# Attention scores of two heads: each head's products on its own 64 partitions, the two heads' banks alternated block by block, keys copied once

## The reference, cut to what matters

```
scores = jnp.einsum('bhqd,bhkd->bhqk', q, k) * scale
attn = jax.nn.softmax(scores + causal, axis=-1)      # sparsemax in the last layer
ctx = jnp.einsum('bhqk,bhkd->bhqd', attn, v_c)
```

## Time and profile before

| what | before |
|---|---|
| median of three runs | 3157.74 us (3154.28 to 3167.81) |
| the profiled execution | 3140.92 us, span 3139.4 us |
| busy share of the span | PE 89%, PEld 72%, DVE 70%, ACT 51%, POOL 48% |
| mean granted TensorE clock | 0.958 of full speed |
| instructions | PE 20990, DVE 6269, ACT 3388, POOL 2213 |

### The profile page before, as it was taken

The page is one execution under the profiler, slowest core; times in us unless marked ns, Lnnn a source line. Parts: engine busy times, 40 slices in busy tenths (PEclk is TensorE's granted clock), DMA queues, the critical chain, the costliest instruction groups (busy, mean ns, idle before and its releaser), DMA issues. The chain is left out here.

```text
span 3139.4 us, 61420 instructions
## 1 busy us (share of the span) xinstructions
PE 2800.3 (89%) x20990; PEld 2273.6 (72%) x20990; DVE 2186.6 (70%) x6269; ACT 1613.7 (51%) x3388; POOL 1513.7 (48%) x2213
## 2 busy tenths in 40 slices
PE   3878699999999999969988889898799999999996
PEld 2555478889899889846666666666588888888864
DVE  4787778788788778757787777766645555454576
ACT  1545444444454444545665555565455555555553
POOL 3587853443343353385656666322233333332487
PEclk8878799999999999989999999999899999999998
DMA  2465678788888888422334343210466666666345
GB/s 82 158 237 178 225 258 311 282 289 307 286 290 308 289 291 309 169 40 55 95 98 107 105 107 106 94 67 23 162 207 215 221 217 212 204 240 203 125 95 125
DMA packets 212009, 580.14 MB, mean 185 GB/s; under 512 B 24617, under 2 KB 146417, under 8 KB 167409
## 3 DMA queue, kind: packets, MB, share of 16 engines
q1 hardware_dynamic: 174832, 525.03, 47.7%
q0 software_dynamic: 36864, 51.14, 8.0%
HBM read 450.14 MB, written 125.96 MB: 184 GB/s over the span
## 5 line engine op out<-in xcount | busy, mean ns | idle before, releaser
L1173 POOL TENSOR_TENSOR al<-t,ah 128x512 fp32r<-128x512 f32 x220 | 284.2, 1292 | 879.3 <-ACT ah L1407 879.3
L544 PE MATMUL bank<-xh,gu 128*128 128x256 f32 x3520 | 675.8, 292 | 33.6 <-DVE gc L1678 25.0
L544 PEld LDWEIGHTS bank<-xh,gu 128*128 128x128 f32 x3520 | 516.1, 191 | 57.6 <-issue 53.8
L1864 DVE TENSOR_REDUCE st<-bank 128x1 f32<-128x512 f32 (+3 forms) x1024 | 421.7, 480 | 157.6 <-PE bank L605 151.8
L1504 ACT ACTIVATE pt<-bank 128x512 f32<-128x512 f32 (+1 forms) x1152 | 510.9, 540 | 25.6 <-PE bank L608 22.9
L587 PE MATMUL bank<-masks_bf,ident_bf 128*128 128x128 bf16 x1896 | 431.2, 251 | 101.0 <-DVE st L1864 38.3
L605 PE MATMUL bank<-ksT,qsT 128*128 128x512 f32 (+3 forms) x1536 | 409.8, 368 | 5.6 <-DVE top L1862 3.1
L1512 ACT ACTIVATE oT<-bank 128x512 f32<-128x512 f32 x192 | 114.6, 597 | 574.4 <-PE bank L684 574.4
L587 PEld LDWEIGHTS bank<-masks_bf,ident_bf 128*128 128x128 bf16 x1896 | 169.9, 98 | 311.1 <-DVE st L1864 96.3
L608 PE MATMUL bank<-qaT,ksT 128*128 128x512 f32 (+3 forms) x1536 | 389.2, 370 | 0.0
L544 PE MATMUL bank<-xl,gu 128*128 128x256 f32 x1760 | 353.5, 282 | 0.0
(11 more groups left out here) (254 smaller groups left out, 5266.9 us busy)
## 6 DMA issues: line engine op xcount, KB each, us to landing
gu<-wu_scratch SPq DMA_DIRECT2D x110, 1032.0 KB, 5.1
gu<-wu_scratch SPq DMA_DIRECT2D x110, 1024.0 KB, 7.4
dn<-wd_scratch SPq DMA_DIRECT2D x110, 1024.0 KB, 6.6
xs<-xs_scratch SPq DMA_DIRECT2D x110, 264.0 KB, 4.4
ys_scratch<-yb SPq DMA_DIRECT2D x110, 256.0 KB, 6.9
raw<-in_gu SPq DMA_DIRECT2D x16, 1024.0 KB, 6.7
wu_scratch<-hi SPq DMA_DIRECT2D x16, 1024.0 KB
wu_scratch<-lo SPq DMA_DIRECT2D x16, 1024.0 KB
```

What stands on the lines that cost most here:

```text
L544: mm = pe.matmul(bank[:, TS * h:TS * (h + 1)], gu[:, col:col + P], x[s % 2][:, TS * k:TS * (k + 1)], start=(n == 0), stop=(n == len(terms) ...
L1173: pool.tensor_tensor(em["al"][s % 2][:, m, :], em["t"][g % 2][:, :], em["ah"][s % 2][:, m, :].bitcast(F32), ALU.subtract).then_inc(al_read ...
L1864: ins = dve.reduce_max(st[:, 0, r:r + 1], bank[:, first:first + width], AX.X)
```

## The change

1. The unit tables are interleaved: both heads' 512-wide units, then both heads' 384 + 128 units, then both 256-wide ones.
2. `scores` takes units two at a time (`both`): it waits for both banks, adds both masks, and then issues the products block by block, head 0 and head 1 in turn, each into its own bank, and each with the 64 rows of its own head (`rows`).
3. The calls in pairs with experts take two units and then four (`FORE = 2`) where they took three and three, on PE, ACT and DVE alike.
4. `ksT` is one tile for each pair without zero rows, filled by one copy of 128 rows on ACT; the semaphore `k_half` and four memsets of the setup go.
5. `masks_last` is asked by the place in the plan; it holds for the q form of the same pairs. With it the masks follow each couple of units, where they followed each three.
6. POOL's `clear` waits for the last two units, one for each head.

```diff
-for _j in range(2):
-    Q_UNITS += [[(_j, 3, 0, 512)], [(_j, 2, 0, 384), (_j, 0, 384, 128)], [(_j, 1, 0, 256)]]
-    K_UNITS += [[(_j, 0, 0, 512)], [(_j, 3, 0, 128), (_j, 1, 128, 384)], [(_j, 2, 0, 256)]]
+for _q, _k in (([(3, 0, 512)], [(0, 0, 512)]),
+               ([(2, 0, 384), (0, 384, 128)], [(3, 0, 128), (1, 128, 384)]),
+               ([(1, 0, 256)], [(2, 0, 256)])):
+    Q_UNITS += [[(_j, *_b) for _b in _q] for _j in range(2)]
+    K_UNITS += [[(_j, *_b) for _b in _k] for _j in range(2)]
 NU = len(Q_UNITS)
+FORE = 2
...
-                    for u in units:
-                        name = (which, G, u)
-                        S.add(name, "dve" if which == "q" else "act")
-                        if S.former[name]:
-                            pe.wait_ge(*S.former[name])
...
+                    for u in units[::2]:
+                        both = (u, u + 1)
+                        for v in both:
+                            name = (which, G, v)
+                            S.add(name, "dve" if which == "q" else "act")
+                            if S.former[name]:
+                                pe.wait_ge(*S.former[name])
                         if not bare and not masks_last:
-                            mask(u, True)
...
+                            for v in both:
+                                mask(v, True)
+                        last_mm = {}
+                        for n in range(len(table_of[u])):
...
+                            for v in both:
+                                j, blk, first, width = table_of[v][n]
+                                rows = slice(SW * j, SW * (j + 1))
+                                to = S.bank((which, G, v))[:, first:first + width]
+                                if which == "q":
+                                    last_mm[v] = pe.matmul(to, mem["qsT"][rows, P * blk:P * (blk + 1)],
+                                                           keys[rows, 0:width], start=begin, stop=end,
+                                                           skip_group_check=True)
...
-                    scores("k", G, range(NU // 2))
+                    scores("k", G, range(FORE))
...
-                    pool.wait_ge(s_act, S.count[("k", G, NU // 2 * (j + 1) - 1)])
+                    pool.wait_ge(s_act, S.count[("k", G, NU - 2 + j)])
...
-                    act.activation(keys[0][0:SW, :], bank[0:SW, :], ACT.Copy).then_inc(k_half, 1)
-                    act.activation(keys[1][SW:P, :], bank[SW:P, :], ACT.Copy).then_inc(x_act, 1)
+                    act.activation(mem["ksT"][key_at[G] % 2][:, :], X.bank(f"Tk{G}")[:, :], ACT.Copy).then_inc(x_act, 1)
```

More of the change, by code:

```diff
@@ L578, in scores @@
                     mem = mems[kinds[G // NP]]
+                    keys = mem["ksT"][key_at[G] % 2]
                     bare = which == "k" and G in plan
-                    masks_last = which == "q" and len(S.banks) == len(units)
+                    masks_last = which == "q" and G - 1 in plan
                     side = 0 if which == "q" else 1
+                    table_of = Q_UNITS if which == "q" else K_UNITS
                     def mask(u, start):
-                        unit = (Q_UNITS if which == "q" else K_UNITS)[u]
+                        unit = table_of[u]
                         diag = min(first + (P * blk if which == "q" else 0) for _, blk, first, _ in unit)
@@ L598, in scores @@
                         if not bare and not masks_last:
-                            mask(u, True)
-                        for n, (j, blk, first, width) in enumerate(unit):
+                            for v in both:
+                                mask(v, True)
+                        last_mm = {}
+                        for n in range(len(table_of[u])):
                             begin = n == 0 and (bare or masks_last)
[L602 to L614, removed]
+                            end = n == len(table_of[u]) - 1 and not masks_last
+                            for v in both:
[6 more added lines that the diff above has]
+                                                           skip_group_check=True)
+                                else:
+                                    last_mm[v] = pe.matmul(to, keys[rows, P * blk:P * (blk + 1)],
+                                                           mem["qaT"][rows, T - width:T], start=begin, stop=end,
+                                                           skip_group_check=True)
@@ L616, in turn_rows @@
+                        for v in both:
+                            if masks_last:
+                                last_mm[v] = mask(v, False)
+                            last_mm[v].then_inc(s_full, 1)
                 def turn_rows(n):
@@ L666, in keys_in @@
                     pe.wait_ge(x_act, X.count[f"Tk{G}" if key_pair(G) == G else f"Tq{G}"])
-                    pe.wait_ge(k_half, key_at[G] + 1)
                 def outputs(G):
@@ L809, in pair_with_experts @@
                         turn_rows(n + 1)
-                    scores("k", G, range(NU // 2, NU))
+                    scores("k", G, range(FORE, NU))
                     if is_at(n - 1, "spm") and p == 1:
@@ L1550, in pair_with_experts @@
                     experts(G, 0)
-                    probabilities(G, range(NU // 2))
+                    probabilities(G, range(FORE))
                     highs()
@@ L1556, in pair_with_experts @@
                         take_rows(n + 1)
-                    probabilities(G, range(NU // 2, NU))
+                    probabilities(G, range(FORE, NU))
                     if is_at(n - 1, "spm") and p == 1:
@@ L2304, in build @@
         "qsT": at("qsT", [P, T], F32R),
-        "ksT": [[at(f"ksT{i}{j}", [P, T], F32R) for j in range(2)] for i in range(2)],
+        "ksT": [at(f"ksT{i}", [P, T], F32R) for i in range(2)],
         "qaT": at("qaT", [P, T], F32R),
```

14 lines of the change are left out of this document (5 added, 9 removed).

## The result

The changed kernel takes 3428.43 us (median of 4 runs, 3423.27 to 3432.94) against 3156.95 us (median of 4): a ratio of **1.0857**, 95% interval 1.0843 to 1.0871.

What follows compares the result with a forecast made beforehand. PE's queue was taken to bound the expert stages and gqa; 70 + 76 + 119 - 25 - 25 = +215 us on the median 3157.7 gave 3373 us, ratio 1.068, range 3250 to 3465.

Steps and rivals of the forecast that it cites:

- What bounds it: PE's queue sets the time in mla with experts, spm with experts and gqa; PE busy 29.8 of 31.3 us in mla.
- Pairs alone, +70: Waits for readers before the third couple and tiling changes: k form +0.41, q form +0.35 us, times 92 pairs.
- spm with experts, +76: Last couple waits for the bank just filled: k form +1.18, q form +0.78 us, times 39 pairs.
- mla with experts, +119, less 25 for `gc`: PE waits for late readers, 4.1 us times 29 pairs; PE's 25.0 us wait for `gc` should vanish in exchange.
- Copies of keys, -25: One ACT copy fewer per key tile, counted only where PE waits: 0.59 us off each of 42 waits.
- mla alone, counted as nothing: 21 pairs where DVE and POOL are as busy as PE (264.1 of 345.4 us): no effect counted.
- Change of tiling: Between 128-row masks and 64-row products: 0.18 us in, 0.09 out, 0.10 load laid open, from 8-row matmuls.
- Full overlap of row halves: Both heads' products on 64 rows run at once, saving 1280 columns of streaming, 0.53 us a form.
- rival of serial halves: Row halves run one after another in the couples: 57 + 20 us more, giving 3450; chance 0.12.
- free changes: Tiling changes cost nothing at 64 rows: 80 + 37 us less, giving 3256; chance 0.11.
- slack: Waits in pairs with experts fall into slack: 170 us would go, leaving about 3200; chance 0.05.
- the faster side: Halved streaming in 384 forms (205 us) and 25 for copies, with no wait in exchange: 2930; chance 0.06.

Runs made afterwards that it cites:

- e6: Kernel with both mends (e5), but in pairs alone the q form's first four masks stand ahead of both couples: 3189.44 us, ratio 1.0106.
- e9: Kernel with both mends (e5), but each mask added in two passes on the head's own 64 rows: 3177.29 us, ratio 1.0054.
- e5c: Kernel with both mends (e5), but the keys' copy done in two halves of 64 rows: 3221.12 us, ratio 1.0193.
- e10: Kernel with both mends (e5), but outputs between the couples only from pair 50 on, so not in mla alone: 3196.44 us, ratio 1.0112.
- e2: Kernel before, with its order and calls, but products of 64 rows and one copy of keys: 3610.51 us, ratio 1.1507.
- e1: Changed kernel's order and calls, but products of 128 rows on padded keys with two key copies: 3343.88 us, ratio 1.0666.
- e12: Kernel with both mends (e5), but products of 128 rows on padded keys with two key copies: 3163.54 us, ratio 1.0021.
- e3: Changed kernel, but with experts three units a call (couple and single, then single and couple), masks behind each q-form call: 3231.63 us, ratio 1.0314.
- e8: Kernel before, with outputs moved in pairs alone behind the fourth unit of q and k forms, as in e4: 3162.82 us, ratio 1.0014.
- e4: Changed kernel, but in pairs alone outputs (q form) and transposes of outputs (k form) stand ahead of the third couple: 3326.81 us, ratio 1.0623.
- e5: Changed kernel with both mends, those of e3 and e4 together: 3188.28 us, ratio 1.0091.

## Why the prediction was right, and where its sizes were off

The forecast was 3373 us, the result 3428.43: the sign, the mechanism and the range held, the sum was +215 and the truth +271. That the range held is in part luck: the two things that the forecast had left out, the clock and mla alone, each put some 27 us on top, and nothing in the range had been set aside for either. Step by step:

**What bounds it.** PE's queue in the stages with experts and in gqa. Confirmed for the stages with experts: PE's idle time there grew by 140 us, where the three rows of waits are 159 and the waits for `gc` became 15 shorter. In pairs alone e6 and e9 show that DVE is close behind.

**Pairs alone, +70.** Measured: gqa +55.4, the stretches of 14 +21.1, the pairs between +0.6, so +77. The medians over gqa, from a form's first start to the next operation's, are 2.73 us for q and 2.56 for k (forecast 2.63 and 2.45), and 2.35 and 2.03 before. ACT's first read of a k form comes 0.81 us after the form's start by the median, forecast 0.84. In the k form shown it has the copy `oT` (0.60 us) ahead of `pt` and begins at 1.31. The 1.93 us that the prediction sets against 1.39 as reading are the moment of release, counted from the form's start; the reading itself is 1.09.

**spm with experts, +76.** Measured +68.7. The second calls take 1.73 us (k) and 2.07 (q) on the mean, forecast 1.88 and 2.20; the first ones 0.44 and 0.54, forecast 0.58 and 0.67. The four calls of a pair take 4.78 us together where they took 3.46 (the same places in the trace of before, 0.66 a k call and 1.07 a q call on the mean), and 1.32 x 39 is 51 us; the other 17 lie outside these calls and were not taken apart.

**mla with experts, +119, less 25 for `gc`.** The stage grew by 118, net. Second calls 2.25 (k) and 3.09 us (q), forecast means 2.4 and 3.4, the first ones 0.43 and 0.53: 6.30 us where 2.96 were, and 3.34 x 29 is 97 us. The waits for `gc` fell by 15, not 25. The clock was 0.96 in this stage where it had been 0.99, by which its 865.5 us of PE work would take 865.5 x (0.99/0.96 - 1) = 27 us more, an estimate; PE was in fact busy 42 us longer. So the forms were over-sized and the clock not seen. The net term, 119 - 25, was short by 24 us.

**Copies of keys, -25.** The waits that name the copy fell from 31.5 to 15.1 us, not below 10 as was forecast, so by these waits the term is 16 us and not 25. By e5c, though, the 160 copies are worth 33 us in the mended kernel, of which only 19 are in waits that name them. The step that was too narrow is "count only where PE waits for the copy". A copy also delays what stands behind it in ACT's queue; that the rest lies there is likely and was not shown.

**mla alone, counted as nothing.** +27 us, of which part is scatter, as e10 says.

**Change of tiling.** I took 0.18 in, 0.10 of load laid open and 0.09 out, from 8 rows. At 64 rows the medians over gqa tell it cleanly (us from start to start):

| step | 128 rows | 64 rows | kernels |
|---|---|---|---|
| one mask of 128 columns to the product | 0.039 | 0.160 | before, e2 |
| one mask of 256 columns to the product | 0.039 | 0.213 | before, e2 |
| product of 512 columns to the next mask | 0.322 | 0.434 | before, e2 |
| couple of 512, both heads, to the next mask | 0.552 | 0.434 | e1, after |
| the second product of a couple behind the first | 0.315 | 0.003 | e1, after |

In: 0.12 to 0.17, out: 0.11, together 0.23 to 0.29 where I had up to 0.37. The Trainium skill, "TensorEngine Tiling", Key Properties, says that a change of mode drains the engine; the trace is in keeping with it, and this table is what a change costs here. e9 confirms it from the other side: with masks on 64 rows the couple of 512 goes to the next mask in 0.322 us, 0.11 less.

**Full overlap of row halves.** It holds: a couple takes as long as one of its products alone, 0.434 us. The rival of serial halves is out, as are free changes (the table), slack (the stages with experts grew by 187 us, 140 of it PE standing idle) and the faster side. The Trainium skill, "TensorE: Matmul & The Clock Gate", Part 3, has tiles on different row groups start about 4 ns apart; here it is 3.

**What I did not see: at once is also late.** Take the steps of gqa's forms in the changed kernel and in e1, the same order on 128 rows, with their waits left out: three couples of masks and three of products in turn (medians; where a step ends in a wait, the same step of a kernel in which it does not, e2's single products for 64 rows and e12's couples for 128). A k form on 64 rows is 0.216 + 0.434 + 0.323 + 0.486 + 0.202 + 0.315 = 1.98 us, on 128 rows 0.094 + 0.551 + 0.150 + 0.659 + 0.081 + 0.322 = 1.86; a q form is 0.205 + 0.434 + 0.322 + 0.430 + 0.202 + 0.316 = 1.91 against 0.084 + 0.552 + 0.148 + 0.702 + 0.081 + 0.411 = 1.98. So the overlap pays for the changes of tiling in the q form, and not in the k form.

And the first bank of a couple is full later, since both fill together behind the change of tiling: ACT's first read of gqa's k forms comes 0.81 us after the form's start, 0.67 in e1, 0.63 before; DVE's in the q forms 0.78, 0.64, 0.61. All that waits for that reader is later by as much. This is the likely reason for most of the distance between 10.95 us a gqa pair in the changed kernel and 10.38 in e1: the medians of the forms are longer by 0.15 (q) and 0.26 (k), 26 of the 36 us. The rest is in keeping with the clock, 0.93 against 0.97: the outputs, 1.20 us by the median in both, took over 1.8 us in 17 of 64 pairs, and in 7 of e1's. It was argued from these starts, not tested alone.

## What to carry to other kernels

Before two streams are interleaved on a ring of banks, count the units between a bank's filling and its next use: four units on a ring of three put a wait for the reader, 0.8 us in the forms shown, on PE in every form, and taking or covering these waits gave back 7.7 of the 8.6%. Splitting the calls so that each bank waited for was filled in the call before took most of it back. Row halves at once save streaming and are paid for with changes of tiling around every mask; from these figures one would expect them to win where the passes between changes are long, and where PE, not the reader of its banks, sets the pace. No run here shows such a win: even e9, with no change of tiling inside a form, is 0.5% above the kernel before.

## What the hardware showed that was not expected

The granted clock changed, and e1 separates two things that go with it. Its windows of mla alone, mla with experts and gqa, products of 128 rows in the changed order:

```profile
56.90:405.00 348.10, 264.73 (x1597) 190.06 (x1595) 261.63 (x762) 165.15 (x329) 259.11 (x297) 0.80 0.51 182
405.00:1429.50 1024.50, 901.33 (x7045) 826.95 (x7044) 740.76 (x1668) 445.09 (x880) 378.23 (x482) 0.96 0.72 258
1591.40:2255.70 664.30, 566.67 (x4286) 410.72 (x4286) 492.27 (x1542) 385.59 (x868) 338.84 (x518) 0.97 0.35 95
```

mla with experts has 0.96 here as in the changed kernel, and 1.00 in e3: that loss goes with the waits. mla alone has 0.80 here, as before (0.81), and 0.74 in the changed kernel: that loss goes with the 64 rows. The other kernels say the same, 0.71 to 0.76 on 64 rows (e2 to e6, e9, e10) and 0.78 and 0.80 on 128 (e8, e12). In gqa it takes both: 0.97 in e1 and before, 0.93 in the changed kernel, 0.94 in e3, which keeps those waits, but 0.96 in e4, which has the 64 rows and covers them; e5 has 0.96 there, and e8 and e12 on 128 rows 0.96 and 0.97. In e2, whose 64-row products run one head at a time, the clock in gqa was lowest; its windows of mla alone, mla with experts and gqa:

```profile
56.60:445.60 389.00, 366.97 (x1595) 233.67 (x1595) 263.15 (x762) 160.26 (x308) 261.14 (x300) 0.71 0.48 170
445.60:1367.90 922.30, 896.07 (x7044) 807.85 (x7043) 733.04 (x1668) 419.91 (x851) 376.82 (x480) 0.99 0.79 284
1564.90:2481.30 916.40, 908.17 (x4286) 557.41 (x4285) 500.30 (x1542) 402.59 (x836) 333.52 (x518) 0.77 0.25 68
```

In gqa PE is busy in 99% of the window and yet gets 0.77. Part of a k form there, in PE's timeline:

```profile
1901.03 2.34 PE L683 MATMUL bank<-pt,V 128*17 128x512 f32 x16
1903.30 0.29 PE L587 MATMUL bank<-masks_bf,ident_bf 128*128 128x128 bf16 x1
1903.52 0.79 PE L608 MATMUL bank<-qaT,ksT 64*128 64x512 f32 x1
1904.24 0.39 PE L587 MATMUL bank<-masks_bf,ident_bf 128*128 128x256 bf16 x1
```

The outputs take 2.27 us where the earlier trace rows have 1.20, and a product of 512 columns 0.72 to the next mask where the same kernel has 0.434 at full speed: this is the level of 1.2 GHz. The kernel goes in and out of it through gqa. So a PE that is never idle, on 64 rows without a partner, was given the slower level for part of the time; with the partner beside it (after, e5) the clock in gqa was 0.93 and 0.96, with masks on 64 rows as well (e9) 0.97. That e2 is dearer than was expected has two parts. At the upper level its steps for three units, 0.160 + 0.434 + 0.214 + 0.163 + 0.323 + 0.160 + 0.314 us, make a k form of 3.54 us, where 3.1 was expected. On top of it comes the lower level: the outputs took over 1.8 us in 31 of 64 pairs. What in the work sets the clock was not tried further.
